# Summing the softmax rows on VectorE instead of in the exponentials' accumulators

## What is computed

```
scores = einsum('bthd,bshd->bhts', q, k) + NEG_INF * (1 - causal)
attn = softmax(scores, axis=-1)
ctx = einsum('bhts,bshd->bthd', attn, v).reshape(B, T, H * Dv)
out = ctx @ Wo + bo
```

## Time and profile before

| | us |
|---|---|
| median of 3 runs | 1592.21 |
| lowest and highest of them | 1584.35, 1595.37 |
| the profiled execution | 1589.19 |
| its span, first to last instruction | 1587.5 |

### The profile page before, as it was taken

The page is one execution under the profiler, slowest core; times in us unless marked ns, Lnnn a source line. Parts: engine busy times, 40 slices in busy tenths (PEclk is TensorE's granted clock), DMA queues, the critical chain, the costliest instruction groups (busy, mean ns, idle before and its releaser), DMA issues. The chain is left out here.

```text
span 1587.5 us, 34224 instructions
## 1 busy us (share of the span) xinstructions
PE 1327.4 (84%) x11168; PEld 1077.3 (68%) x11168; DVE 1021.0 (64%) x2723; ACT 876.1 (55%) x3255; POOL 834.0 (53%) x996
## 2 busy tenths in 40 slices
PE   2879797989899998989888998989889898986550
PEld 1667676777777776777777776867767777765540
DVE  3566657566756777667766767666776767666233
ACT  3656555565665665565655656565655655553120
POOL 4353334553446546664566545664566545564345
PEclk9999899999999999999999999999999999999685
DMA  6000000032112212132122212133122222133651
GB/s 211 8 7 8 7 8 14 10 92 81 36 57 69 84 57 60 47 105 85 36 63 83 81 54 65 44 94 95 36 65 76 81 64 64 33 95 104 183 156 46
DMA packets 142897, 105.78 MB, mean 67 GB/s; under 512 B 12352, under 2 KB 137856, under 8 KB 142720
## 3 DMA queue, kind: packets, MB, share of 16 engines
q1 hardware_dynamic: 132224, 84.71, 18.3%
q0 software_dynamic: 8192, 16.79, 3.6%
q10 hardware_dynamic: 2304, 2.10, 0.4%
HBM read 69.99 MB, written 33.55 MB: 65 GB/s over the span
## 5 line engine op out<-in xcount | busy, mean ns | idle before, releaser
L1595 POOL TENSOR_TENSOR pr<-pr,ri 128x480 f32<-128x480 f32 x256 | 250.4, 992 | 267.3 <-DVE ri L1229 265.3
L919 ACT ACTIVATE pr<-sE,nm 128x120 f32<-128x120 f32 x512 | 177.6, 359 | 292.1 <-DVE nm L1215 292.1
L591 PE MATMUL pvb<-pT,vv 120*64 120x128 f32 x2048 | 143.2, 283 | 42.9 <-DVE pT L1225 42.6
L919 ACT ACTIVATE pr<-sO,nm 128x120 f32<-128x120 f32 x512 | 178.8, 381 | 0.0
L558 PEld LDWEIGHTS sE<-kT,qT 64*128 64x128 f32 x1024 | 127.7, 193 | 54.8 <-issue 54.8
L591 PEld LDWEIGHTS pvb<-pT,vv 120*64 120x64 f32 x2048 | 112.5, 139 | 72.5 <-DVE pT L1225 55.3
L1635 POOL DMA_INDIRECT gat<-sorted_y,slot x128 | 127.1, 993 | 64.3 <-issue 47.1
L1623 POOL DMA_INDIRECT sorted_x<-x,slot x128 | 128.1, 1001 | 49.4 <-issue 34.6
L558 PE MATMUL sE<-kT,qT 64*128 64x120 f32 x1024 | 151.6, 290 | 0.0
L558 PE MATMUL sO<-kT,qT 64*128 64x120 f32 x1024 | 151.6, 290 | 0.0
L417 PE MATMUL t<-ident_f,pr 128*120 128x128 f32 x1024 | 146.6, 290 | 1.8 <-POOL pr L1595 1.4
(11 more groups left out here) (334 smaller groups left out, 3535.5 us busy)
## 6 DMA issues: line engine op xcount, KB each, us to landing
wq<-in_w_e SPq DMA_DIRECT2D x224, 128.0 KB
sorted_y<-yq SPq DMA_DIRECT2D x64, 256.0 KB, 2.5
xq<-sorted_x SPq DMA_DIRECT2D x56, 256.0 KB, 2.8
xt<-in_x SPq DMA_DIRECT2D x16, 256.0 KB, 3.0
sorted_x<-yq SPq DMA_DIRECT2D x16, 256.0 KB, 4.0
out_y<-y SPq DMA_DIRECT2D x64, 64.0 KB, 1.6
cT<-in_ctxT SPq DMA_DIRECT2D x16, 240.0 KB, 3.0
sorted_x<-x,slot POOLq DMA_INDIRECT x128
```

Of the source, the lines that this page charges most:

```text
L591: ins = mm(pvb[r * DK:(r + 1) * DK, (k // 2) * T:(k // 2 + 1) * T], vv[:, q, h * DK:(h + 1) * DK], pT[:, 4 * r + k // 2, :], start=True, s ...
L919: ins = f(pr[:, p % RING, r, i, :], score_banks[r][:, i * S:(i + 1) * S], ACT.Exp, bias=nm[:, p % 2, r, i:i + 1], accum_out=rsum[:, p % 2, ...
L1595: GP.tensor_tensor(pr[:, p % RING, r, :, :], pr[:, p % RING, r, :, :], ri[:, p % 2, r, :, :].to_broadcast([P, 4, S]), ALU.mult).then_inc(s ...
```

## The change

The exponentials no longer write an accumulator. In their place VectorE reduces pr of both banks in one operation (128 x 8 x 120 elements to 8 sums) and takes one reciprocal of 8 values. It waits for the exponentials of bank sO, for the products of pair p-2 on GpSimd (whose ri it overwrites), and for its own sums. GpSimd's two products of a pair now both wait for this one reciprocal. The semaphore rinv counts to 8 in a group instead of 16, rsum is new, and tri1 of the preamble is merged with ones.

```diff
@@ ScalarE
                 for i in range(4):
                     ins = f(pr[:, p % RING, r, i, :], score_banks[r][:, i * S:(i + 1) * S], ACT.Exp,
-                            bias=nm[:, p % 2, r, i:i + 1], accum_out=rsum[:, p % 2, r, i, :])
+                            bias=nm[:, p % 2, r, i:i + 1])
                 ins.then_inc(sem["probs"], 1)
@@ VectorE
-            def b_recips(b, p, r):
-                dve.wait_ge(sem["probs"], upto("probs", b, 2 * p + r))
-                V.reciprocal(ri[:, p % 2, r, :, :], rsum[:, p % 2, r, :, :]).then_inc(sem["rinv"], 1)
+            def b_recips(b, p):
+                dve.wait_ge(sem["probs"], upto("probs", b, 2 * p + 1))
+                if p > 1:
+                    dve.wait_ge(sem["normal"], upto("normal", b, 2 * p - 3))
+                elif later(b):
+                    dve.wait_ge(sem["normal"], upto("normal", b - 1, 2 * (PAIRS + p) - 3))
+                V.tensor_reduce(rsum[:, p % 2, :, :, 0], pr[:, p % RING, :, :, :], AX_X, ALU.add).then_inc(sem["rsum"], 1)
+                dve.wait_ge(sem["rsum"], upto("rsum", b, p))
+                V.reciprocal(ri[:, p % 2, :, :, :], rsum[:, p % 2, :, :, :]).then_inc(sem["rinv"], 1)
@@ VectorE, body
                     if B and s < PAIRS:
-                        b_recips(b, s, 0)
-                    if B and s < PAIRS:
-                        b_recips(b, s, 1)
+                        b_recips(b, s)
@@ GpSimd
-            GP.memset(tri[:], 1.0).then_inc(sem["tri1"], 1)
-            pool.wait_ge(sem["tri1"], 1)
+            GP.memset(tri[:], 1.0).then_inc(sem["ones"], 1)
+            pool.wait_ge(sem["ones"], 2)
@@ GpSimd
             def b_normal(b, p, r):
-                pool.wait_ge(sem["rinv"], upto("rinv", b, 2 * p + r))
+                pool.wait_ge(sem["rinv"], upto("rinv", b, p))
```

More of the change, by code:

```diff
@@ L70 @@
     "ctx_hi": 1, "ctx_split": 1, "proj": 24, "proj_act": 12, "proj_dve": 12, "scores": 16, "negmax": 16, "probs": 16,
-    "probsT": 16, "probsT0_sb": 8, "probsT1_sb": 8, "rinv": 16, "normal": 16, "pv": 8, "headsT_sb": 8,
+    "probsT": 16, "probsT0_sb": 8, "probsT1_sb": 8, "rsum": 8, "rinv": 8, "normal": 16, "pv": 8, "headsT_sb": 8,
     "wo": 4, "attn_sum": 4, "ln2_stats": 4, "ln2_mv": 4, "ln2_eps": 4, "ln2_rstd": 4, "ln2_out": 4,
@@ L91 @@
 ONCE = ["waits_held", "mixer_weights", *[f"{n}_in" for n in LATE_LOADS], "w_hi", "w_lo", "ident", "identb", "mask0", "mask", "iota", "iotaf", "ones", "gammas", "bq8", "powers", "pads",
-        "tri1", "tri", "onesb", "zeros", "xs_zeroed",
+        "tri", "onesb", "zeros", "xs_zeroed",
         "xq_last0", "xq_last1", "wq_last0", "wq_last1", "wq_last2", "wq_last3"]
```

## The result

The changed kernel takes 1648.3 us (median of 6 runs, 1643.3 to 1651.3), the kernel before 1592.5 in the same comparison: a ratio of 1.035, with a 95% interval of 1.033 to 1.038. The forecast was 1658 us, slower. The cost forecast was 67 us, and 56 us were measured. The profiled execution has a span of 1643.6 us, against 1587.5.

A forecast was written before the change was run, and what follows sets the result against it. A loop between VectorE's maxima and ScalarE's exponentials was taken to bound the kernel. Groups 3 to 15 gave 54 us, routing work 8, groups 0 to 2 4.5: 67 us on 1589.2, 1658 us with the median's 3; range 1620 to 1705.

The forecast's parts named there:

- the loop: VectorE's maxima, ScalarE's exponentials, VectorE's reciprocals, its work behind them, next maxima; said to set the time in steps 2 to 7.
- The loop's part: Reduction behind the exponentials, 1.30 us for 0.12, less 0.75 us on ScalarE: 1.96 us a group, summed over steps 2 to 7.
- Steps 3, 4 and 7: Pair steps of a group: +0.43 us each in 3 and 7, +0.24 in 4, where VectorE already waited for ScalarE's tanh.
- Step 2: Second pair step of the loop's stretch in a group: an idle of 0.28 us before ssf closes too, so about 0.
- steps 5 and 6: Pair steps of a group: +0.43 us each; 6 counted as an odd step since its heads copy ends late.
- The routing work: Eight groups (c_slots) where steps 0 and 1 don't hide: +0.35 and +0.43 us, 8 x 1.0 = 8 us in the sum.
- The first three groups: Groups 0 to 2, little behind the reciprocals, part of 0.75 us gained where scores were last: 3 x 1.5 = 4.5 us.
- The products' place: Both GpSimd products back to back behind the reciprocal, delaying VectorE's small SBUF work: 2.2 us a group in groups 3 to 15.
- holding: VectorE's small SBUF operations delayed while a GpSimd product runs: 0.9 to 6.3 us a group, 2.2 taken.
- The rival of the loop alone: Only the loop lengthens, with no more holding than today: 35 us, 1625 us; chance 0.2.
- The rival that VectorE's work hides: VectorE's idle time covers the reduction and the exponentials' 0.75 us counts: 41 us faster, 1551 us; chance 0.03.
- That of the clock: More TensorE idle brings more 1.2 GHz stretches; shared case with everything behind both products: 1680 to 1725 us, chance 0.2.

The follow-up runs named there:

- the exchange: Accumulator reads replaced by the reduction: the changed kernel (ratio 1.035) against one keeping accumulators, without reduction, both products behind one reciprocal (ratio 1.023).
- short products: GpSimd's products cut from 120 to 8 columns of each head: 1568.2 us in the changed kernel, 1556.4 us in the kernel before.
- one-reciprocal kernel: Changed kernel with accumulators kept and no reduction, one reciprocal for both banks and both products behind it: 1625.5 us, ratio 1.023 to the kernel before.
- the square: Four kernels, both products behind one reciprocal: accumulator reads only 1625.5 us, reduction only (changed kernel) 1648.3, both 1726.2, neither 1545.3.

## Why the prediction was right, and where its sizes were off

The direction held, and so did the two mechanisms: VectorE is late in the loop, so an added 1.18 us counts there although the engine idles a third of the time, and moving GpSimd's products costs more again than the exchange itself. The sum of 67 us against 56 is nearer than its two terms, which missed in opposite ways; that part is luck. Point by point:

- The prices. Reduction 1.15 us forecast, 1.151 measured. Exponentials 0.25 us apart, 0.24 measured. The stretch from one pair's end to the next maxima, +1.18 forecast, +1.20 measured. The added wait for the products of pair s-2 is on no list of waits of the changed kernel.
- The loop's part. 13 x 1.96 + 8 x 0.78 and 4.5 for the first groups are 36 us. The exchange measured 20, and 12 to 17 with short products. The term that was mis-sized is the sum by steps, which let the exponentials' 0.75 us and the 1.18 us on VectorE count in the same pairs. Steps 3, 4 and 7 came out near it (+0.3, +0.4, +0.3). Step 2 was put at 0 and gained 0.3, since the reads cost 0.7 there and the reduction only 0.4, and steps 5 and 6 have 0.1 and 0.2 in place of 0.43. The routing work was counted in eight groups, but the eighth turn with it comes after the last pair (its cast starts at 1473.8 us in the kernel before, the last maxima at 1442.9), so seven have pairs beside it. The first three groups lost 1.8 us each in the changed kernel, where I had put 1.5, but as +2.0 in step 3 and +1.8 in the last, and -1.4 in step 6. The +2.0 goes with TensorE's waits for xn in step 3 (2.3 us in groups 0 and 1).
- The products' place. 13 x 2.2 and 8 x 0.2 are 30 us. Measured it is 36 (one reciprocal against the kernel before), but holding is only 22 of them (67 less 45), and 12 in the changed kernel. Steps 2 and 4 came out near the forecast: 0.6 us, where 0.5 was put on ssf, and 0.8, where 0.9 was put on y and keep (it is all keep). In step 6 I had y held by another 0.4 us. It is not held any more; in its place VectorE waits for the scores of pair 7, the 12 us more that go with the lower clock. In the changed kernel ssf takes at most 0.43 us, and y's mean fell from 435 to 398 ns, because it now gets in between two products. TensorE's waits for xn were on none of my lists, and its stretches at 1.2 GHz only in a rival.
- So the loop was put some 16 us too high and the products' place 6 too low: 67 forecast, 56 measured.
- Of the signs that I had named, VectorE's wait for ScalarE fell (114.2 to 48.9), ScalarE's wait for nm rose (292.1 to 363.5), and the period of a group rose from 90.1 to 94.4 us (groups 5 to 15). VectorE's wait for the scores did not fall (49.7 to 52.0 us): in groups 3 to 15 the 5.7 us before pair 1 are gone, but those before pair 7 rose from 9.8 to 18.6. Y and ssf over 1 us was wrong.
- The rival of the loop alone (1625 us) is refuted by the one-reciprocal kernel, which has no longer path on VectorE and is at 1625 by the products alone. The rival that VectorE's work hides is refuted by the square. That of the clock has a part in the time: it shows at pair 7, and its whole share stays open.

## What to carry to other kernels

An operation's price depends on whether its engine is the late one at that place, not on its busy share: read who waits for whom between two dependent engines, and put the added work into the wait (bank sE's sum under bank sO's exponentials) rather than behind it, and see that the wait is as long as the work in every turn. When a result that another engine waits for comes later, follow that engine too: what it does next, and whom it holds while it does it. And look for the engine that waits in every turn; here ScalarE took half of GpSimd's products into its wait, and the kernel gained 29 us.

## What the runs showed of the hardware that I had not expected

An accumulator read is listed at 0.20 to 0.23 us but keeps ScalarE for 0.09 us only; taking 1024 of them away lowered the engine's busy time, which counts overlapped time once, by 92 us (876.1 to 784.4), and the kernel's time by 78 to 83 us where the exponentials are in the loop. And 112 of the 120 columns of GpSimd's products cost the kernel before 35 us of its 1592, about as much as VectorE's operations were held by them: GpSimd itself was busy for 53% and did not look like a bound.
